# One launch of conditioning, attention, adapter and int8 feed-forward: batch 0's after-attention work and batch 1's preparation spread over three head groups each

## The reference, cut to what matters

```python
h   = x @ cond_W[cid] + cond_b[cid]                 # 512 x 512
q, k, v = split(h @ w_qkv.T)                        # 16 heads of 32
s   = q k^T / sqrt(32) - |i - j| * slope[head]      # causal, masked with -1e4
num = 0.5 * (1 + s * rsqrt(1 + s*s));  prob = num / (sum(num) + 1e-6)
x1  = x + (prob @ v) @ w_out.T
a   = relu(x1 @ W1[lid] + b1) @ W2[lid] + b2        # 512 -> 128 -> 512
z   = layernorm(x1 + a) * gamma[lid] + beta[lid]
out = x1 + int8_matmul(quantize(z, one scale from max|z| of both batches), w8) * scales + bias
```

## Time and profile before

| | us |
|---|---|
| runs | 2186.1, 2194.39, 2194.62 (median 2194.39) |
| the profiled execution | 2191.51 |
| its span, first to last instruction | 2189.8 |
| mean granted TensorE clock, share of full | 0.929 |

### The profile page before, as it was taken

One profiled execution on the slowest core, in us unless ns is written; L12 is line 12 of the kernel. 1 busy time (PEld: TensorE's weight loads), 2 busy tenths in 40 slices (PEclk: granted clock), 3 DMA queues, 4 the chain that ended last, 5 costly groups with the idle time before them and its releaser, 6 DMA issues.

```text
span 2189.8 us, 29394 instructions
## 1 busy us (share of the span) xinstructions
PE 1778.5 (81%) x10699; PEld 901.2 (41%) x10702; DVE 1736.8 (79%) x1730; ACT 1709.5 (78%) x1842; POOL 1693.0 (77%) x723
## 2 busy tenths in 40 slices
PE   5678888888887879997786887888888788988764
PEld 4455434333333445654343443433333344444231
DVE  4248888988999878977555777899999898879748
ACT  0037999999999978977554777999999998889652
POOL 3037899999989968877554776899998998889648
PEclk9899999999999989999988999999999999999889
DMA  5411111111111112212211212011111113112146
GB/s 182 150 50 41 46 31 31 42 38 35 36 35 45 31 56 64 60 41 61 68 44 47 81 50 64 24 44 40 36 32 36 41 31 90 42 57 58 59 160 204
DMA packets 122139, 130.38 MB, mean 60 GB/s; under 512 B 27372, under 2 KB 77548, under 8 KB 121580
## 3 DMA queue, kind: packets, MB, share of 16 engines
q1 hardware_dynamic: 121996, 128.51, 21.0%
HBM read 45.89 MB, written 22.54 MB: 31 GB/s over the span
## 4 chain that ended last, share of the span: by engine, by line
PE 34%; ACT 28%; DVE 17%; issue 11%; POOL 4%; SPq 3%; DMA 2%; DVEq 0%; POOLq 0%; ACTq 0%
ACT yb L765 11%; ACT gb L730 8%; ACT yb L767 8%; DVE gb L1094 6%; PE sc L943 6%; PE ov L921 6%; DVE gb L1159 5%; PE dn L921 5%; PE it L859 4%; PE it L866 4%; PE it L839 3%; SPq L479 3%; POOL oT L724 2%; PE it L843 2%; DMA area<-in_x_dram 1%
## 5 line engine op out<-in xcount | busy, mean ns | idle before, releaser
L691 POOL TENSOR_TENSOR yb<-yb 128x1024 f32<-128x1024 f32 x544 | 1503.6, 2776 | 384.8 <-DVE gb L1159 369.0
L1159 DVE TENSOR_TENSOR gb<-sc,yb 128x1024 f32<-128x1024 f32 x544 | 663.3, 1219 | 170.2 <-ACT yb L767 165.6
L765 ACT ACTIVATE yb<-sc 128x1024 f32<-128x1024 f32 x544 | 550.7, 1012 | 265.0 <-PE sc L943 157.9
L1094 DVE TENSOR_TENSOR gb<-gb,yb 128x1024 f32<-128x1024 f32 x544 | 753.8, 1386 | 0.0
L943 PE MATMUL sc<-qmv,kst 128*128 128x512 f32 (+3 forms) x1280 | 479.7, 458 | 175.0 <-DVE gb L1159 160.7
L767 ACT ACTIVATE yb<-yb 128x1024 f32<-128x1024 f32 x544 | 575.6, 1058 | 17.2
L730 ACT ACTIVATE gb<-gb 128x1024 f32<-128x1024 f32 x544 | 566.2, 1041 | 0.0
L943 PEld LDWEIGHTS sc<-qmv,kst 128*128 128x128 f32 x1280 | 230.6, 202 | 492.9 <-DVE gb L1159 342.8
L921 PE MATMUL ov<-gb,vv 128*32 128x512 f32 (+3 forms) x2560 | 320.0, 584 | 30.2 <-DVE den L1108 22.6
L921 PE MATMUL dn<-gb,ones 128*32 128x512 f32 (+3 forms) x2560 | 310.5, 568 | 0.0
L839 PE MATMUL it<-hT,wT 128*128 128x512 f32 x496 | 249.4, 608 | 14.4 <-ACT area L742 8.5
(11 more groups left out here) (118 smaller groups left out, 1087.9 us busy)
## 6 DMA issues: line engine op xcount, KB each, us to landing
qmv<-stage SPq DMA_DIRECT2D x384, 64.0 KB
kst<-stage SPq DMA_DIRECT2D x384, 64.0 KB
area<-in_x_dram SPq DMA_DIRECT2D x58, 256.0 KB, 2.8
out_dram<-oT SPq DMA_DIRECT2D x32, 256.0 KB, 3.2
wT<-wT_d SPq DMA_DIRECT2D x7, 768.0 KB, 4.3
x_d<-area SPq DMA_DIRECT2D x16, 256.0 KB, 2.6
z_d<-area SPq DMA_DIRECT2D x16, 256.0 KB, 2.9
gb<-z_d SPq DMA_DIRECT2D x4, 1024.0 KB, 12.2
```

The lines of the kernel that those rows point to most:

```text
L691: pool.tensor_tensor(y, y, y, ALU.mult).then_inc(s_y2, 1)
L765: act.activation(yview(n), sc[:, n % SLOTS], ACT.Square).then_inc(s_s2, 1)
L1094: dve.tensor_tensor(gview(n), gview(n), yview(n), ALU.add).then_inc(s_num, 1)
L1159: dve.tensor_tensor(gview(n), sc[:, n % SLOTS], yview(n), ALU.mult).then_inc(s_g, 1)
```

## The change

Two DRAM tensors are added, `h_d` and `o_d`. The h of batch 1 is no longer written into `hT`: DVE writes it to a two-place buffer `hst`, SP stores it to `h_d`, and loads it back by chunks (1 MB each): chunks 0 and 1 at the start of closing, chunk 2 behind closing's last reader of it (v 2), chunk 3 behind v 3 and the last h. So batch 1's tiles are made in three groups: tiles 0 to 5, 6 to 11 and 12 to 15. The attention output of batch 0 is stored to `o_d` by chunk when its norm is done (1 MB each), and "o" jobs take it from there by tile into a two-place buffer `otl` in `oT`. So after-work of batch 0 is in three groups: tiles 0 to 4, 5 to 10 and 11 to 15. The four plain groups are replaced. `EVAC` goes from 1 to 2 and `NORMED` from 2 to 3, but the ending group keeps 1 and 2 for its after-jobs. A rule is added to the planner (except in ending): a job that isn't due stays back until the last-but-one job placed is two pairs old.

```diff
-EVAC = 1
-NORMED = 2
+EVAC = 2
+NORMED = 3
@@ Group.__init__, the loop that places jobs
                     if t[0].parts and left < 0.5 * t[0].parts[0] and t[0].end > k:
                         break
+                    full = [job for job in order if job.parts][-BANKS:]
+                    if not tight and t[0].parts and t[0].end > k and len(full) == BANKS and full[0].at + 2 > k:
+                        break
@@ the groups
-    closing = Group(NC, [job for j in range(KB)
-                         for job in cond_jobs(j, 2 if j < TT else first[j // TT] + 1, first[NC] - 24 + j)], True, slack=0.7)
-    joining = Group(NC, [job for j in range(KB) for job in joined(j)], True, slack=1.5)
+    def made_early(tiles, until):
+        return [job for j in tiles for job in cond_jobs(j, 4, until)]
+    spare_a = Group(NC, made_early(range(0, 6), PAIRS - 4), True, slack=0.5)
+    spare_b = Group(NC, made_early(range(6, 12), PAIRS - 4), True, slack=0.5)
+    closing = Group(NC, made_early(range(12, KB), first[3] - 1), True, slack=0.5)
+    def done_late(tiles, start):
+        return [job for j in tiles for job in after_jobs(j, start, PAIRS - 4, PAIRS - 2)]
+    joining = Group(NC, done_late(range(0, 5), 8), True, slack=0.7)
+    late_a = Group(NC, done_late(range(5, 11), 1), True, slack=0.7)
+    late_b = Group(NC, done_late(range(11, KB), 1), True, slack=0.7)
     ending = Group(NC, [... after_jobs(j, first[j // TT + 1] + LAG + NORM, first[NC] - 9 + j - KB + TT,
-                        first[NC] - 1)], False, slack=1.0)
+                        first[NC] - 1, 1, 2)], False, slack=1.0, tight=True)
-        return ([(0, opening if b == 0 else joining)] + [(hg, plain) for hg in range(1, NG - 1)] +
-                [(NG - 1, ending if b == B - 1 else closing)])
+        return list(enumerate((opening, spare_a, spare_b, closing) if b == 0 else (joining, late_a, late_b, ending)))
@@ SP
+            def load_made(c):
+                sp.dma_start(hT[:, :, chunk], h_d[:, :, chunk]).then_inc(s_hl, 16)
+            def keep_outputs(c):
+                sp.wait_ge(s_norm, (NG - 1) * NC + c + 1)
+                sp.dma_start(o_d[:, :, chunk], oT[:, :, chunk]).then_inc(s_ost, 16)
+            def load_outputs(j):
+                sp.wait_ge(s_ost, 16 * max(3, j // TT + 1))
+                sp.dma_start(otl[:, j % 2], o_d[:, :, j * P:(j + 1) * P]).then_inc(s_otl[j % 2], 16)
@@ SP, behind "o"
+                    if b == 0 and j + 2 < KB:
+                        sp.wait_ge(s_item, i + 1)
+                        load_outputs(j + 2)
@@ SP, group()
+                if g is spare_a:
+                    sp.wait_ge(s_evac, dve_base)
+                    cond_weights(1, cids[1])
+                    for j in range(2):
+                        load_x(1, j)
                 if g is closing:
                     sp.wait_ge(s_evac, dve_base)
-                    cond_weights(b + 1, cids[b + 1])
-                    for j in range(2):
-                        load_x(b + 1, j)
+                    for a in range(2):
+                        sp.wait_ge(s_hst[a], 16 * 6)
+                    for c in range(2):
+                        load_made(c)
...
+                    elif what == "h" and g is not opening:
+                        sp.wait_ge(s_evac, dve_base + rank)
+                        sp.dma_start(h_d[:, :, c * P:(c + 1) * P], hst[:, c % 2]).then_inc(s_hst[c % 2], 16)
+                    elif what == "n" and (g is joining if len(e[1].name) == 3 else g is closing):
+                        keep_outputs(c)
@@ PE
+                            pe.wait_ge(s_otl[j % 2], 16 * (j // 2 + 1))
+                            if g is closing and e[1].name == ("q", 0, "next"):
+                                pe.wait_ge(s_hl, 32)
+                            elif g is joining and e[1].name in (("q", 2), ("q", 3)):
+                                pe.wait_ge(s_hl, 16 * (e[1].name[1] + 1))
@@ DVE
+                    if b:
+                        dve.wait_ge(s_hst[a], 16 * (c // 2))
-                    dve.tensor_tensor(hT[:, :, tok], feat,
+                    dve.tensor_tensor(hst[:, a] if b else hT[:, :, tok], feat,
+                if G == NG:
+                    dve.wait_ge(s_ost, 16 * (c + 1))
```

More of the change, by code:

```diff
@@ L135, in __init__ @@
         self.has_next = has_next
[L137 removed]
+        made = {}
         for job in others:
[L139 to L140 removed]
+            if job.name[0] == "h" and opens:
+                made.setdefault(job.name[1] // TT, []).append(job)
         f, end = self.first, len(self.pairs) - 1
@@ L221, in adaln_attn_ffn @@
     first = plain.first + [len(plain.pairs)]
+    UNITS, PAIRS = len(plain.units), len(plain.pairs)
     opening = Group(NC, [job for j in range(TT, KB)
                          for job in cond_jobs(j, first[j // TT - 1], first[j // TT] - (12 if j >= 2 * TT else 5))], True, True, 1.5)
-    closing = Group(NC, [job for j in range(KB)
-                         for job in cond_jobs(j, 2 if j < TT else first[j // TT] + 1, first[NC] - 24 + j)], True, slack=0.7)
[L230 to L234, removed]
-    joining = Group(NC, [job for j in range(KB) for job in joined(j)], True, slack=1.5)
-    assert all(job.at <= first[job.name[1] // TT + 1] + LAG - 2 for job in joining.items if job.name[0] == "o")
+    def made_early(tiles, until):
[8 more added lines that the diff above has]
+    late_b = Group(NC, done_late(range(11, KB), 1), True, slack=0.7)
+    LATE = (joining, late_a, late_b)
     DONE = KB - TT - 2
     ending = Group(NC, [job for j in range(DONE) for job in
-                        after_jobs(j, first[j // TT + 1] + LAG + NORM, first[NC] - 9 + j - KB + TT, first[NC] - 1)], False, slack=1.0)
-    UNITS, PAIRS = len(plain.units), len(plain.pairs)
+                        after_jobs(j, first[j // TT + 1] + LAG + NORM, first[NC] - 9 + j - KB + TT, first[NC] - 1, 1, 2)], False, slack=1.0, tight=True)
     TOTAL = B * NG * PAIRS
@@ L350, in adaln_attn_ffn @@
         s_wt = sem("s_wt")
+        s_hst = [sem(f"s_hst_{i}") for i in range(2)]
+        s_hl = sem("s_hl")
+        s_ost = sem("s_ost")
+        s_otl = [sem(f"s_otl_{i}") for i in range(2)]
         s_item = sem("s_item")
@@ L458, in zs_before @@
         def zs_before(b, j):
-            order = [job.name[1] for job in (ending if b == B - 1 else joining).items if job.name[0] == "zt"]
+            order = [job.name[1] for g in ((ending,) if b == B - 1 else LATE) for job in g.items if job.name[0] == "zt"]
             n = KB * b
@@ L600, in group @@
                         operand("qk".index(what), c, nhg)
+                    elif what == "v" and c == 2 and g is closing:
+                        sp.wait_ge(s_item, base + item + 1)
+                        load_made(c)
                     elif what == "v" and c == NC - 1 and g.has_next:
@@ L607, in group @@
                         sp.wait_ge(s_item, base + item + 1)
-                        load_x(b if g is opening else b + 1, c + 2)
-                    elif what in ("o", "zt"):
-                        after(b if g is ending else b - 1, e[1], base + item, (act_base if what == "zt" else dve_base) + rank)
+                        load_x(batch_of(g, e[1].name), c + 2)
+                    elif what == "h" and g is not opening:
[3 more added lines that the diff above has]
+                        keep_outputs(c)
+                    elif what in ("o", "zt"):
+                        after(batch_of(g, e[1].name), e[1], base + item, (act_base if what == "zt" else dve_base) + rank)
+                    if g is closing and item == made_at:
+                        for a in range(2):
+                            sp.wait_ge(s_hst[a], 16 * 8)
+                        load_made(NC - 1)
                     item += 1
@@ L701, in group @@
                     elif e[0] == "step":
-                        after(b if g is ending else b - 1, e[1], base)
+                        after(batch_of(g, e[1].name), e[1], base)
                 if k is not None:
@@ L770, in group @@
                     for job in after_pair.get(k, []):
-                        d = b if g is ending else b - 1
+                        d = batch_of(g, job.name)
                         after(d, job, bases[0] + job.index, zs_before(d, job.name[1]))
@@ L862, in compute @@
                     if part == 0:
-                        pe.wait_ge(s_norm, ((b + 1) * NG - 1) * NC + j // TT + 1)
+                        if b == B - 1:
+                            pe.wait_ge(s_norm, ((b + 1) * NG - 1) * NC + j // TT + 1)
+                        else:
+                            pe.wait_ge(s_otl[j % 2], 16 * (j // 2 + 1))
                         if j == 0:
                             pe.wait_ge(s_bw, 16 * 7 * (b + 1))
-                    r = pe.matmul(bank, oT[:, part, tok], woT[:, part, :], **ends)
+                    o = oT[:, part, tok] if b == B - 1 else otl[:, j % 2, part, :]
+                    r = pe.matmul(bank, o, woT[:, part, :], **ends)
```

(2 more changed lines are left out.)

32 lines of the change are left out of this document (23 added, 9 removed).

## The result

The changed kernel takes 2077.98 us (median of 5 runs, 2068.65 to 2081.35), against 2191.18 us before (5 runs); the ratio is 0.9474, 95% interval 0.9453 to 0.9495. The profiled execution took 2068.65 us, span 2066.9 us, granted clock 0.947. It is the fastest of the five, so its difference to the profiled execution of before, 122.9 us, is about 10 us more than that of the medians.

The account below looks back on a forecast made before the run. ACT was taken to bound plain groups, PE closing, waits between engines joining. From 2191.5 us, after-work's 105.9 and conditioning's 17 came off, the rest zero: 2068.6, stated as 2070, range 2034 to 2118.

Parts of the forecast that it names:

- After-work: Batch 0's 16 tiles in joining, late_a and late_b: 3.2 us a tile, three groups 680.0 us, gain 105.9.
- ending's quiet 22 pairs: Ending from pair 39 on, 84.9 us: 20.0 us for about 6.25 tiles, giving the 3.2 us a tile used.
- the bound of 4.0: Upper bound in us per after-work tile, from all of ending, where 10 tiles cost 39.9 us.
- The route by the planner's budget: Second estimate for after-work groups: 47 pairs at closing's 3.50 us plus 21 at 2.95, again 680 in sum.
- ACT's share as a lower bound: After-work groups: ACT's 2.4 us a tile can't be hidden where ACT has the pace.
- Lags and rule: Chain o, rt, a, w2, zt: with lags of 2 and 3 pairs, tiles should find their evacuations done.
- the 54 of the rival: After-work groups: joining's chain waits return, 3.35 us a tile, 54 us over 16; the prediction's version gave 2122, chance 0.09.
- Conditioning: Batch 1's 16 tiles in spare_a, spare_b and closing: 1.1 us a tile, sum 650 us, gain 17.
- the wait of 4 us for x: Start of spare_a: about 4 of PE's 10.45 us wait for the first x tile would stay.
- Stores and loads: Added SP transfers, 20 us of issue over six groups: priced at zero, hidden by distance; bounds 0 and 45 us.
- the slower rival: Six middle groups: SP's added waits make q and k operands late, 144 us of loss, 2213 us; chance 0.03.
- Opening and ending: The first and last head groups: zero change each, with bounds of 5 us to either side.

Follow-up runs that it names:

- e3: Changed kernel with only batch 0's after-work spread, batch 1's h made in closing as in the kernel before; 2096.15 us, ratio to before 0.9559.
- e4: Changed kernel with only batch 1's conditioning spread, all batch 0 after-work in joining as in the kernel before; 2167.61 us, ratio to before 0.9889.
- e7: Changed kernel with late_a's planner budget at 0.8 instead of 0.7; 2070.24 us, ratio to before 0.9451, one run of 5306.63 us left out.
- e12: Changed kernel with late_a's budget at 0.8 once more, beside the unaltered changed kernel on the same chip; 2073.01 us, ratio to before 0.9458.
- e6: Changed kernel with zt evacuated by one 512-column activation instead of four of 128, altering the computation; 2072.78 us, ratio to before 0.9447.
- e9: Changed kernel with two of four feature blocks left out of batch 0's o (64 of 128 matmuls); 2071.69 us, ratio to before 0.9469.
- e10: Changed kernel with half an o for batch 0 and one activation for each zt; 2061.07 us, ratio to before 0.9419.
- e13: Changed kernel with VectorE's layernorm statistics and largest-|z| search over 128 of 512 columns; 2069.18 us, ratio to before 0.9432.
- e1: Changed kernel with spreading, but the planner's lags back at 1 and 2 pairs and no two-pairs rule; 2087.65 us, ratio to before 0.9533.
- e2: Kernel before with the longer lag and two-pairs rule, nothing spread, joining and ending exempt; 2204.22 us, ratio to before 1.0051.
- e5: Changed kernel with every added transfer accompanied by a second of the same size; 2074.31 us, ratio to before 0.9465.
- e11: The changed kernel itself, run again as reference on the same chip; 2074.46 us, ratio to before 0.9481.

## Why the prediction was right

**Where the time was.** The prediction put all of the gain into what the six middle groups had above the plain mean, 195.6 us, less the price of the same work there. The chip agrees in place: 116.1 of the 122.9 us between the profiled executions come from these groups, and e3 and e4 give the two halves apart.

**After-work.** Forecast 3.2 us a tile and 680.0 us for the three groups; measured (692.9 - 628.8) / 16 = 4.0 and 692.9. This is the term that was mis-sized, by 12.9 us. Of these, 10.5 are in late_a, forecast at 228 and measured at 238.5; joining took 224.3 and late_b 230.1, both forecast at 226. So most of the error goes with the one group of six tiles, and e7 and e12 show that its overdue zt is not the reason. The step that failed is the one that took ending's quiet 22 pairs as nearest and left out the crowded ones; the bound of 4.0, from all of ending, was the measured value. The route by the planner's budget made the same 680 and was no second witness: it took closing's pace, from a group with no after-work in it, for 47 pairs.

**ACT's share as a lower bound.** The bound of 2.4 us a tile was not broken (4.0 came), but the reason given for it, that ACT has the pace and its share can't be hidden, does not hold in the late groups: e6 took 10.4 us of ACT's work away for 0.6. No number of the sum stood on it. What the late groups have is four engines at 87 to 92% (by the changed kernel's sum row PE 202, DVE 211, ACT 212, POOL 207 us of a mean 231). By e6, e9, e10 and e13 none of them alone sets the time, and VectorE's part reached it most. GpSimd's work was cut in no run, so its share is open. A busy share is not all work, either: e1 has the same VectorE instructions in its late groups and 611.1 us of busy time where the changed kernel has 633.2, because its adds took 1.36 us on average instead of 1.49.

**Lags and rule.** The prediction left the chain's waits out because the lags double. Right: idle ahead of after-work fell from 68.1 us to 6.7 over the 16 tiles. e1 shows the price without them, 16 us in the late groups and not the 54 of the rival: with the old lags a tile's matmuls wait 1.7 us when five or six tiles share a group, where they waited 3.35, the weights left out, with 16 in one. e2 shows that the longer lag and the rule without spreading don't pay.

**Conditioning.** Forecast 650 us (a gain of 17), measured 644.2 (23.1). A tile cost (644.2 - 628.8) / 16 = 0.96 against 1.1, and the wait of 4 us for x at the start of spare_a did not come. In the changed kernel SP issued the operand's 12 DMAs from 353.64, before the group's first pair at 354.8, where closing's had begun 3 us into the group:

```profile
353.64 7.74 SPq L498 DMA_DIRECT2D qmv<-stage  x12
363.18 7.52 SPq L486 DMA_DIRECT2D area<-in_x_dram  x4
```

The second row is the x loads, four of them; the first transposition began at 369.3 with no wait. The step that failed here was to take SP's start in closing for its start in spare_a.

**Stores and loads.** They were priced at zero, and e5 agrees. No wait of PE for `otl` or for the reloaded `hT`, and none of DVE for `hst`, stands in the waits view. The score matmuls' waits for operands are 11.8 and 1.4 us, 13.2 in all against 13.0 before. Taken to the letter that is 0.2 us past the mark of 13 that the prediction set, but it is no change, and the slower rival, operands behind the new waits of SP, has nothing. A trip's 2.6 and 3.1 us for 256 KB agree with the about 2 us of fixed cost in the Trainium skill's DMA: Bandwidth & Descriptors, section on the anatomy of one DMA, though that section is on transfers issued by GpSimd and these are issued by SyncE. That the trips stand in line, the waits view and e5 exclude.

**Opening and ending.** Zero was taken, and -0.7 and -2.2 us came. Opening's is scatter: in e11 the same opening took 269.3 us, against 265.3. The 4.3 us behind ending were in no step, and no run isolates them.

**The total.** 2068.6 was worked out for an execution like the profiled one, and that took 2068.65; but three terms are off (after-work +12.9, conditioning -6.1, the rest -6.8) and cancel. That the two agree to 0.1 us is luck. The median is 8 us above the 2070 forecast. Of the signs named, five of the six groups lie between 212 and 232 us; late_a's 238.5 does not, just under the 240 that would have counted against the account. PE's idle ahead of rt, a, w2 and zt was 0.4 us a tile, under 1 as named. The wait of 4 us for x was a sign too, and it did not appear.

## What to carry to other kernels

Read a long kernel by stage, take the best stage as the yardstick, and price moved work where it goes: the gain is what the crowded stages have above the yardstick less a price per unit, and both ends of that price were in the profile (ending's 4.0 was the one that came, probably since the new stages are mixed like all of ending, and not quiet). Distance between dependent steps paid here where there was room (e1) and cost time where there was none (e2). Where four engines are all near 90% busy, a cut on one can be given back almost whole, as those on PE and ACT were here; try each, and two together, before calling a stage bound by one.

## What the runs showed of the hardware that was not expected

One ACT activation of 512 columns with one scale took 760 ns in e6, four of 128 columns took 449 ns each (1.49 us from first to last, as they overlap). A 1 MB store from `oT` landed in 4.5 us, a 1 MB load into `hT` in 6.3 us, in the fence of e5. GpSimd's squaring, 2.83 us in the first plain group before, took 2.72 us in joining after, with VectorE's add at 1.49 us instead of 1.36. The two mean times move in opposite directions. The add's mean hides single ones of 1.21 us and others of up to 2.90 in the late groups; no run took it apart.
